# The third layer's attention: adding up the scan's states on POOL instead of DVE

## The chip, the cores and the metric

The kernel runs on one core of one Trainium2 chip. The metric is the device time of one execution in microseconds; three executions of the kernel before took 1468.19 us in the median (1460.56 to 1477.25). One more execution was recorded by the profiler; all rows in this document come from that one.

Engines are called as in the profile: PE (TensorE), PEld (its weight loads), DVE (VectorE), ACT (ScalarE), POOL (GpSimd), SP (SyncE, which issues DMAs here).

## What is computed

A stack of four layers on `x` of shape 4 x 256 x 256. Each layer adds a gated attention-like block and then a gated feed-forward block:

```python
x = x + jnp.tanh(g_xattn[1]) * _L1_xattn_ref(ctx_1024, _layernorm(x, axis=-1), ...)   # a state-space scan
x = x + jnp.tanh(g_ffn[1])   * _L1_ffn_ref(...)
x = x + jnp.tanh(g_xattn[2]) * _L2_xattn_ref(_layernorm(x, axis=-1), ctx_1024, ...)   # 16 heads of attention
x = x + jnp.tanh(g_ffn[2])   * _L2_ffn_ref(...)
x = x + jnp.tanh(g_xattn[3]) * _L3_xattn_ref(ctx_1024, _layernorm(x, axis=-1), ...)   # a second scan
x = x + jnp.tanh(g_ffn[3])   * _L3_ffn_ref(...)
```

The scan in layers 2 and 4 (`L1_`, `L3_`) depends on the context `ctx_1024` and its weights alone; only a gate at its end reads `x`:

```python
def step(state, inp):
    d, b, c, u = inp
    dA = jnp.exp(d[..., None] * A)
    state = state * dA + (d * u)[..., None] * b[:, None, :]
    y = jnp.einsum('bdn,bn->bd', state, c)      # 16 states n are summed for each channel d
    return (state, y)
y = y + D[None, :, None] * x
```

The attention of the third layer (`L2_xattn`) has 16 heads of width 128, 4 batches of 256 queries and 256 keys, with an RMS norm of queries and keys:

```python
q = rmsnorm(q, gq); k = rmsnorm(k, gk)
scores = jnp.einsum('bqhd,bkhd->bhqk', q, k) * scale
out = jnp.einsum('bhqk,bkhd->bqhd', jax.nn.softmax(scores, axis=-1), v)
return out.reshape(B, Sq, H * D) @ Wo
```

## The kernel before

There is no scheduler. Each engine has its own program, written out in order, and the engines meet at semaphores; a semaphore wait holds up all that stands behind it on its engine. What runs beside what is thus fixed by the order in which the lines stand and by the waits.

Since the last layer's scan needs nothing of `x`, it is laid into the third layer's attention (`m=1` in the `ssm_` functions). The scan has 32 groups (`GROUPS`): 4 batches x 4 blocks of 4 states x 2 halves of the 256 channels. Group `j` of a batch has block `j // 2` and half `c = j % 2`. A group is a tile of 128 partitions (channels) x 1024, four states (`NB`) by 256 positions (`S`). For each group:

- ACT makes the decays (L457), DVE the inputs by a product (L468), DVE runs the scan (L479, 1024 long);
- POOL multiplies the states by the rows of C (L499, in `ssm_hC`), into one of two buffers `ssm_hC_buf`;
- DVE adds up the four states (L520, a reduction of 1024 to 256 with strided input, into `ssm_part`) and adds the result to `ssm_y` (L524, 256 long). This is `ssm_reduce_dve`.

The attention goes through 64 steps, 16 heads times 4 batches, `step(i, k, b)` on PE, ACT and DVE alike; `h = 4*i + k` is the head. What this text calls **b0 to b3** are the four steps of a head. Each step, in order:

- PE: scores of this step (L1520); transposes of the weights of the step before (L1500); a piece of the next head's projections (keys and values L1442, queries L1451; in b3 the queries' sums of squares L1458 and the transposes of the keys L1466); values of the step before (L1508).
- DVE: row maxima (L1685), their scaled negatives (L1689), in b1 and b3 the scan's input product (L468), after ACT's exponentials (L1627) the reciprocal of the sums (L1695) and the normalization of the weights, two instructions of 128x256 (L1698), the copy of the step before's output (L1668), in b2 the keys' mean squares (L1659), in b3 the queries' (L1664). Then in b1 and b3 the scan; in b0 and b2 `ssm_reduce_dve` for the group whose scan ended the step before.
- POOL, once a head (`head` in `x_pool`): the product L499 of the even group; `rms`, the keys' inverse roots (L1753, 8 columns) and their application to the next head's keys (L1756, 1024 columns); `qrms`, the queries' inverse roots (L1762); the product L499 of the odd group.

The keys of the next head are transposed (L1466) only after L1756, and b0 of the next head can't take its maxima's scale before L1762. PE stands in order: the values of b2 (L1508) are behind that transpose.

Even heads from the third on (h = 2, 4, ..., 14) also carry the output projection of the pair of heads before them (PE L1490: 8 matmul records in b1, 16 in b2, 8 in b3; DVE adds them to `x`, L1674). They are called **projecting heads** below, the others **plain heads**.

The first batch of the scan runs beside heads 0 to 3, and so on. Heads 4 to 11 are a hardware loop on every engine.

Of the kernel before, what the change touches and what calls it, by code (L numbers as in the profile page):

```python
# [55 lines left out]
def flamingo_kernel(nc, A, out):  # L56
    with ExitStack() as ctx:
# [3 lines left out]
        def sem(name):  # L61
            return ctx.enter_context(nc.semaphore(name))
# [220 lines left out]
        s_ssm_y = sem("s_ssm_y")  # L283
        s_ssm_red = sem("s_ssm_red")
        s_ssm_red_y = sem("s_ssm_red_y")
        ssm_part = sb("ssm_part", [P, S])

        prep_groups += [
            ([win_rows[:, m, c, :] for m in range(2) for c in range(HC)], winT[:, :, :].rearrange("p a b -> p (a b)")),
# [220 lines left out]
                                        start=(g == 0 and n == 0), stop=(g == GB - 1 and n == NB - 1))  # L510
            last.then_inc(s_ssm_sum, 1)

        def ssm_reduce_dve(dve, m, b, j):

            c = j % HC
            q = b * GB * HC + j
            dve.wait_ge(s_ssm_hC, m * GROUPS + q + 1)
            if not (isinstance(b, int) and b == 0 and j == 0):
                dve.wait_ge(s_ssm_red_y, q)
            nc.vector.tensor_reduce(ssm_part[:, :], ssm_hC_buf[:, j % 2, :].rearrange("p (n l) -> p l n", n=NB),  # L520
                                    AX_X, ALU.add).then_inc(s_ssm_red, 1)
            dve.wait_ge(s_ssm_red, q + 1)
            row = ssm_y[:, m, ds(b, 1), c, :].rearrange("p a l -> p (a l)")
            nc.vector.tensor_tensor(row, row, ssm_part[:, :], ALU.add).then_inc(s_ssm_red_y, 1)  # L524

        def ssm_sum_dve(dve, m, b):
            dve.wait_ge(s_ssm_sum, m * GROUPS + (b + 1) * GB * HC)
# [17 lines left out]
        def gated_dve(dve, m, k):  # L545

            if m:
                norm_dve(dve, k)
                dve.wait_ge(s_ssm_red_y, GROUPS)
            else:  # L550
                norm_dve(dve, k)
                dve.wait_ge(s_ssm_y, B * HC)
            for b in range(B + 1):
                if b < B:
                    dve.wait_ge(s_z_silu, m * B + b + 1)
                    rows = z_gate[:, TPB * b:TPB * (b + 1), :]
                    nc.vector.tensor_tensor(rows, rows, ssm_y[:, m, b, :, :], ALU.mult).then_inc(s_z_prod, 1)
                if b:
                    dve.wait_ge(s_z_t, m * B + b)
                    rows = x[:, TPB * (b - 1):TPB * b, :].rearrange("p a n -> p (a n)")  # L560
                    nc.vector.scalar_tensor_tensor(out=rows, in0=bank[b % 2][:, :], scalar=tanh_g[:, 0, 2 * m + 1:2 * m + 2],
                                                   in1=rows, op0=ALU.mult, op1=ALU.add).then_inc(s_z_x, 1)
                    norm_stats(dve, range(TPB * (b - 1), TPB * b), s_z_x, m * B + b)
# [807 lines left out]
        x_nb = sb("x_nb", [P, 2, TPB])  # L1371
        x_sum = sb("x_sum", [P, 2, TPB])
        x_inv = sb("x_inv", [P, 2, TPB])
        s_x_g = sem("s_x_g")
        s_x_gqk = sem("s_x_gqk")
        s_x_w = [sem(f"s_x_w{r}") for r in range(2)]
# [6 lines left out]
        def after(eng, sem_, value):  # L1383

            if not (isinstance(value, int) and value <= 0):
                eng.wait_ge(sem_, value)

        def x_sp(sp):
            sp.dma_start(x_gqk[:, 0:1], A["L2_xattn_gq"].rearrange("(p a) -> p a", a=1)).then_inc(s_x_g, 16)
# [260 lines left out]
        def x_dve(dve):  # L1650
            V = nc.vector
            dve.wait_ge(s_x_g, 32)
            V.tensor_tensor(x_gqk[:, 0:1], x_gqk[:, 0:1], x_gqk[:, 1:2], ALU.mult).then_inc(s_x_gqk, 1)
            norm_dve(dve, 4)

            def krms(h):
                dve.wait_ge(s_x_ksq, 4 * h + 4)
                after(dve, s_x_rk, h)
                V.tensor_scalar(x_kve[:, :], x_kss[:, :], 1.0 / P, EPS, ALU.mult, ALU.add).then_inc(s_x_kve, 1)  # L1659

            def qrms(h):
                dve.wait_ge(s_x_ss, h + 1)
                after(dve, s_x_rq, h)
                V.tensor_scalar(x_qve[:, :], bank[2][:, 0:NT], L2_SCALE_EPS, None, ALU.add).then_inc(s_x_qve, 1)  # L1664

            def ocopy(s, r, b):
                dve.wait_ge(s_x_O, s + 1)
                V.tensor_copy(x_OT[:, r, b * S:(b + 1) * S], bank[7][:, 0:S]).then_inc(s_x_Oc, 1)  # L1668

            def add(n, p, at_bank):  # L1670
                dve.wait_ge(s_x_wo, n + 1)
                after(dve, s_x_add, n)
                rows = x[:, 2 * p:2 * p + 2, :].rearrange("p a n -> p (a n)")
                V.scalar_tensor_tensor(out=rows, in0=bank[at_bank][:, :], scalar=tanh_g[:, 0, 2:3], in1=rows,  # L1674
                                       op0=ALU.mult, op1=ALU.add).then_inc(s_x_add, 1)

            def step(i, k, b, first=False, final=False):
                h = i * HB + k
                s = i * (HB * B) + (k * B + b)
                par = b % 2  # L1680
                if b == 0:
                    dve.wait_ge(s_x_rq, h + 1)
                dve.wait_ge(s_x_S, s + 1)
                after(dve, s_x_exp, s - 1)
                V.tensor_reduce(x_top[:, par, :], bank[4 + par][:, :].rearrange("p (t n) -> p t n", t=TPB), AX_X, ALU.max,  # L1685
                                negate=True).then_inc(s_x_top, 1)
                dve.wait_ge(s_x_top, s + 1)
                for t in range(TPB):
                    last = V.tensor_scalar(x_nb[:, par, t:t + 1], x_top[:, par, t:t + 1],  # L1689
                                           x_rq[:, k % 2, TPB * b + t:TPB * b + t + 1], None, ALU.mult)  # L1690
                last.then_inc(s_x_max, 1)
                if par:
                    ssm_in_product(dve, 1, i, 2 * k + b // 2)
                dve.wait_ge(s_x_exp, s + 1)
                V.reciprocal(x_inv[:, par, :], x_sum[:, par, :]).then_inc(s_x_inv, 1)  # L1695
                dve.wait_ge(s_x_inv, s + 1)
                for t in range(TPB):
                    last = V.tensor_scalar(x_P[:, par, t * S:(t + 1) * S], x_P[:, par, t * S:(t + 1) * S],  # L1698
                                           x_inv[:, par, t:t + 1], None, ALU.mult)
                last.then_inc(s_x_P, 1)  # L1700
                if k % 2 == 0 and not (isinstance(h, int) and h < 2) and b == 1:
                    add(2 * h - 4, 0, 3)
                if not first:
                    r, pb = (k if b else k - 1) % 2, (b - 1) % B

                    u = i * (HB // 2) + (k if b else k - 1) // 2
                    after(dve, s_x_wo, 4 * u + (pb - 3))
                    ocopy(s - 1, r, pb)
                if not final:
                    n, r = h + 1, (k + 1) % 2  # L1710
                    if b == 2:
                        krms(n)
                    elif b == 3:
                        qrms(n)
                if k % 2 == 0 and not (isinstance(h, int) and h < 2):
                    u4 = 2 * h - 4
                    if b == 2:
                        add(u4 + 1, 1, 0)
                        add(u4 + 2, 2, 1)
                    elif b == 3:  # L1720
                        add(u4 + 3, 3, 3)
                j = 2 * k + b // 2
                if par:
                    ssm_scan(dve, 1, i, j)
                elif j:
                    ssm_reduce_dve(dve, 1, i, j - 1)
                elif not first:
                    ssm_reduce_dve(dve, 1, i - 1, GB * HC - 1)

            krms(0)  # L1730
            qrms(0)
            for k in range(HB):
                for b in range(B):
                    step(0, k, b, first=(k == 0 and b == 0))
            with dve.Fori(1, H // HB - 1) as i:
                for k in range(HB):
                    for b in range(B):
                        step(i, k, b)
            for k in range(HB):
                for b in range(B):  # L1740
                    step(H // HB - 1, k, b, final=(k == HB - 1))
            ssm_reduce_dve(dve, 1, B - 1, GB * HC - 1)
            after(dve, s_x_wo, 2 * H - 4)
            ocopy(H * B - 1, 1, B - 1)
            for p in range(4):
                add(2 * H - 4 + p, p, p)
                norm_stats(dve, (2 * p, 2 * p + 1), s_x_add, 2 * H - 3 + p)

        def x_pool(pool):
# [13 lines left out]

            def head(i, k, final=False):
                h = i * HB + k
                ssm_hC(pool, nc.gpsimd, 1, i, 2 * k)
                if not final:
                    rms(h + 1, (k + 1) % 2)
                    qrms(h + 1, (k + 1) % 2)
                ssm_hC(pool, nc.gpsimd, 1, i, 2 * k + 1)  # L1770

            rms(0, 0)
            qrms(0, 0)
# [84 lines left out]
                f = stop  # L1858

        def g_sp(sp):  # L1860
            sp.wait_ge(s_ssm_red_y, GROUPS)
            pad = FS2 // P * P
            sp.dma_start(g_wr[:, :], A["L2_ffn_Wr"]).then_inc(s_g_ld[0], 16)
            sp.dma_start(e_gw[:, :], A["L3_ffn_gate_w"]).then_inc(s_g_ld[0], 16)
# [644 lines left out]
```

## Time and profile before

| | |
|---|---|
| median of 3 executions | 1468.19 us (1460.56 to 1477.25) |
| the profiled execution | 1462.29 us, span of its trace 1460.6 us |
| busy over the span | PE 1153.7 us, DVE 905.0, ACT 627.8, POOL 577.9 |
| the attention with the scan in it | from about 540 to 992 us of the span |

The profile lists for each engine when each instruction started, how long it took and, in brackets, how long its engine had been idle before it and whose result ended that wait. The third layer's attention is nearly a third of the span. In it the work of one head comes back every 25 to 30 us, with the same instructions, so a few rows of one plain and one projecting head stand for all sixteen.

### The profile page before, as it was taken

Reading aid. Unit: us, or ns where it says so; the run is one execution under the profiler, and the core shown is the slowest. Engines: PE = TensorE matmul, PEld = TensorE weight load, DVE = VectorE, ACT = ScalarE, POOL = GpSimd, SP = SyncE. Lnnn points to the kernel's source line nnn. Section 1 sums busy time; section 2 is a strip of 40 time slices with the busy share of each in tenths; the row PEclk is TensorE's granted clock in tenths of the full one; section 3 lists DMA queues with packets and bytes.
Section 4 is the critical chain, followed back from the end, with each engine's and each line's share of the span. In section 5 each row is a group of like instructions: output and inputs, shape, how many; then the busy total and the mean of one; then the engine's idle time right before and its main releaser. Section 6 shows DMA issues by size and latency. Waiting matters only on the chain.

```text
span 1460.6 us, 18407 instructions
## 1 busy us (share of the span) xinstructions
PE 1153.7 (79%) x5364; PEld 875.7 (60%) x5365; DVE 905.0 (62%) x1598; ACT 627.8 (43%) x1682; POOL 577.9 (40%) x369
## 2 busy tenths in 40 slices
PE   6755687877448878889889889868999833999993
PEld 3545576665225556667677677646555532888782
DVE  4485998977698625887787888873222366232222
ACT  3382364543711136666666767635111014333331
POOL 1006888888001213343343443420000001788874
PEclk9687899988768987999899999979999956999997
DMA  5664799975300001022021022014600099455556
GB/s 164 158 134 113 206 314 270 267 180 95 115 1 1 29 14 37 30 80 71 11 80 68 12 79 72 2 42 145 159 0 1 10 272 216 86 83 82 82 81 125
DMA packets 130069, 145.61 MB, mean 100 GB/s; under 512 B 29510, under 2 KB 114239, under 8 KB 129991
## 3 DMA queue, kind: packets, MB, share of 16 engines
q1 hardware_dynamic: 104326, 110.05, 25.9%
q0 software_dynamic: 24576, 33.57, 13.7%
q10 hardware_dynamic: 1088, 1.05, 0.2%
q8 instruction: 36, 0.59, 0.2%
q14 instruction: 43, 0.34, 0.1%
HBM read 118.52 MB, written 26.12 MB: 99 GB/s over the span
## 4 chain that ended last, share of the span: by engine, by line
PE 40%; DVE 18%; issue 15%; POOL 9%; ACT 6%; DMA 5%; SPq 5%; DVEq 0%; ACTq 0%; POOLq 0%
PE bank L1904 6%; PE bank L2197 5%; DVE arena L479 4%; PE bank L1913 3%; PE bank L1490 3%; SPq L2083 2%; ACT arena L1627 2%; PE bank L1451 2%; DVE ssm_part L520 2%; POOL x_rq L1762 2%; PE bank L1442 2%; DVE x_top L1685 2%; DMA e_sums<-ctxT,put 2%; PE bank L1508 1%; PE bank L1264 1%
## 5 line engine op out<-in xcount | busy, mean ns | idle before, releaser
L479 DVE TENSOR_TENSOR_SCAN arena<-arena 128x1024 f32<-128x1024 f32 x64 | 146.5, 2289 | 12.4 <-issue 8.3
L499 POOL TENSOR_TENSOR arena<-arena 128x1024 f32<-128x1024 f32 x32 | 75.1, 2348 | 182.3 <-DVE arena L479 182.3
L913 POOL DMA_INDIRECT f_sums<-arena,put x64 | 123.3, 1927 | 24.0 <-issue 17.7
L200 POOL TENSOR_TENSOR rstd<-var_eps,minus_half 128x8 f32<-128x8 f32 x8 | 13.2, 1646 | 299.4 <-DVE var_eps L192 299.4
L1627 ACT ACTIVATE arena<-bank,x_nb,x_rq 128x256 f32<-128x256 f32 x128 | 71.1, 559 | 100.7 <-DVE x_nb L1689 100.7
L899 POOL DMA_INDIRECT arena<-y_rows,slots x64 | 83.2, 1300 | 77.8 <-DVEq L1108 57.6
L2197 PE MATMUL bank<-arena,ssm_y 128*128 x512 | 111.1, 360 | 2.6 <-issue 0.9
L2110 POOL DMA_INDIRECT e_sums<-ctxT,put x64 | 101.6, 1587 | 24.2 <-issue 16.7
L457 ACT ACTIVATE arena<-arena,ssm_A 128x255 f32<-128x255 f32 (+1 forms) x256 | 107.8, 499 | 1.8 <-DVE arena L429 1.8
L1904 PE MATMUL bank<-yT,arena 128*128 128x512 f32 (+1 forms) x224 | 102.4, 600 | 0.0
L509 PE MATMUL bank<-arena,ident 128*128 128x256 f32 x256 | 70.7, 424 | 38.4 <-DVE arena L499 34.0
L2197 PEld LDWEIGHTS bank<-arena,ssm_y 128*128 128x128 f32 x512 | 86.3, 192 | 10.9 <-issue 7.0
L2119 POOL DMA_INDIRECT y<-y_rows,slots x64 | 62.8, 982 | 73.7 <-DMA y_rows<-y 52.9
L2386 DVE TENSOR_SCALAR ctxT<-bank,slot_w 128x256 f32<-128x256 f32 x64 | 31.0, 484 | 94.5 <-DMA e_sums<-ctxT,put 80.2
L509 PEld LDWEIGHTS bank<-arena,ident 128*128 128x128 f32 x256 | 50.8, 207 | 56.1 <-DVE arena L499 36.3
L1508 PE MATMUL bank<-arena 128*128 128x256 f32 x256 | 77.0, 429 | 7.0 <-ACT arena L1617 7.0
L468 DVE TENSOR_TENSOR arena<-arena 128x1024 f32<-128x1024 f32 x64 | 77.9, 1218 | 0.0
L1520 PE MATMUL bank<-arena 128*128 128x256 f32 x256 | 74.6, 418 | 3.8 <-issue 1.6
L1508 PEld LDWEIGHTS bank<-arena 128*128 128x128 f32 x256 | 52.2, 214 | 31.1 <-ACT arena L1617 17.0
L1951 ACT ACTIVATE arena<-bank 128x512 f32<-128x512 f32 (+1 forms) x28 | 16.7, 597 | 122.6 <-PE bank L1904 122.6
L1904 PEld LDWEIGHTS bank<-yT,arena 128*128 128x128 f32 (+1 forms) x224 | 42.6, 191 | 42.9 <-issue 41.5
L1762 POOL TENSOR_TENSOR x_rq<-x_qve,minus_half 128x8 f32<-128x8 f32 x16 | 41.4, 2587 | 65.6 <-DVE x_qve L1664 65.6
(313 smaller groups left out, 2771.9 us busy)
## 6 DMA issues: line engine op xcount, KB each, us to landing
arena<-bc_rows SPq DMA_DIRECT2D x64, 512.0 KB
arena<-in_L_ffn_w_gate_dram SPq DMA_DIRECT2D x16, 256.0 KB
arena<-in_L_ffn_w_up_dram SPq DMA_DIRECT2D x16, 256.0 KB
arena<-in_L_ffn_w_down_dram SPq DMA_DIRECT2D x16, 256.0 KB
x<-in_L_ffn_w_gate_dram SPq DMA_DIRECT2D x16, 256.0 KB, 3.7
y<-in_L_ffn_w_up_dram SPq DMA_DIRECT2D x16, 256.0 KB, 4.0
yT<-in_L_ffn_w_down_dram SPq DMA_DIRECT2D x16, 256.0 KB, 4.6
arena<-in_L_ffn_Wd_dram SPq DMA_DIRECT2D x1, 3072.0 KB, 24.3
```

The lines of the kernel that those rows point to most:

```text
L457: last = nc.scalar.activation(ssm_decay[:, j % 2, n * S + 1:(n + 1) * S], ssm_delta[:, c, ds(b * S + 1, S - 1)], ACT.Exp, scale=ssm_A[:, m ...
L468: nc.vector.tensor_tensor(ssm_in.rearrange("p (n l) -> p n l", n=NB), ssm_B[:, g % 2, :].rearrange("p (n l) -> p n l", n=NB), ssm_du[:, c, ...
L479: nc.vector.tensor_tensor_scan(ssm_h[:, j % 2, :], ssm_decay[:, j % 2, :], ssm_in, 0.0, ALU.mult, ALU.add).then_inc(s_ssm_h, 1)
L499: ops.tensor_tensor(ssm_hC_buf[:, j % 2, :], ssm_h[:, j % 2, :], ssm_C[:, g % 2, :], ALU.mult).then_inc(s_ssm_hC, 1)
L509: last = nc.tensor.matmul(bank[6 + c][:, 0:S], ident[:, :], ssm_hC_buf[:, j % 2, n * S:(n + 1) * S], start=(g == 0 and n == 0), stop=(g == ...
L899: nc.gpsimd.indirect_dma_start(out=f0_xg[:, n % RING, e, :], out_offset=None, in_=y_rows, in_offset=bass.IndirectOffsetOnAxis(ap=slots[:, ...
L913: nc.gpsimd.indirect_dma_start(out=f0_sums[m % SUMS], out_offset=bass.IndirectOffsetOnAxis(ap=put[:, m:m + 1], axis=0), in_=f0_ye[:, n % R ...
L1508: last = nc.tensor.matmul(bank[7][:, 0:S], x_kv[:, NT * r + TPB * b + j, P:2 * P], x_PT[:, b % 2, j * S:(j + 1) * S], start=(j == 0), stop ...
L1627: last = nc.scalar.activation(x_P[:, b % 2, t * S:(t + 1) * S], bank[4 + b % 2][:, t * S:(t + 1) * S], ACT.Exp, bias=x_nb[:, b % 2, t:t + ...
L1904: last = nc.tensor.matmul(bank[2 * (t % 2) + w][0:rows, :], wt[:, c * D + h * rows:c * D + (h + 1) * rows], yT[:, h, n * HALF:(n + 1) * HA ...
L2110: nc.gpsimd.indirect_dma_start(out=e_sums[t % 2], out_offset=bass.IndirectOffsetOnAxis(ap=put[:, t:t + 1], axis=0), in_=e_ye[:, t % 4, :], ...
L2197: last = nc.tensor.matmul(dst, e_xgT[:, r, h * P:(h + 1) * P], src[:, ds(which, 1), h, :].rearrange("p a (w n) -> p (a w) n", w=2), start= ...
```

## The change

The sum over four states goes from DVE to POOL, and is gathered per batch and half in an accumulator `ssm_acc` of 256 columns. Behind each product L499 POOL now adds the upper 512 columns of the buffer to the lower 512, then the two quarters that are left to the accumulator: one addition of 256 for the first block of a batch (`j < 2`), two for the others. DVE adds the accumulators to `ssm_y` once for each batch and half: at the end of b1 of heads 4, 8 and 12, and at the end of the stage. `ssm_part` is gone; `ssm_acc` lies in a part of the arena that the attention doesn't use otherwise. Three waits count 8 additions to `ssm_y` in place of 32.

```diff
+        def ssm_out_pool(pool, m, b, j):
             c = j % HC
             q = b * GB * HC + j
+            ssm_hC(pool, nc.gpsimd, m, b, j)
+            pool.wait_ge(s_ssm_hC, m * GROUPS + q + 1)
+            add = nc.gpsimd.tensor_tensor
+            both = ssm_hC_buf[:, j % 2, 0:2 * S]
+            add(both, both, ssm_hC_buf[:, j % 2, 2 * S:4 * S], ALU.add).then_inc(s_ssm_half[0], 1)
+            after(pool, s_ssm_half, q + 1)
+            parts = ssm_hC_buf[:, j % 2, 0:S], ssm_hC_buf[:, j % 2, S:2 * S]
+            acc = ssm_acc[:, c, :]
+            if j < HC:
+                after(pool, s_ssm_red_y, b * HC)
+                add(acc, parts[0], parts[1], ALU.add).then_inc(s_ssm_red, 1)
+            else:
+                pool.wait_ge(s_ssm_red, q - 1)
+                add(acc, acc, parts[0], ALU.add).then_inc(s_ssm_some[0], 1)
+                after(pool, s_ssm_some, b * (GB - 1) * HC + (j - HC + 1))
+                add(acc, acc, parts[1], ALU.add).then_inc(s_ssm_red, 1)
+
+        def ssm_out_dve(dve, m, b):
+
+            for c in range(HC):
+                dve.wait_ge(s_ssm_red, b * GB * HC + (GB - 1) * HC + c + 1)
+                row = ssm_y[:, m, ds(b, 1), c, :].rearrange("p a l -> p (a l)")
+                nc.vector.tensor_tensor(row, row, ssm_acc[:, c, :], ALU.add).then_inc(s_ssm_red_y, 1)
...
                 if par:
                     ssm_scan(dve, 1, i, j)
-                elif j:
-                    ssm_reduce_dve(dve, 1, i, j - 1)
-                elif not first:
-                    ssm_reduce_dve(dve, 1, i - 1, GB * HC - 1)
+                if b == 1 and k == 0 and not (isinstance(i, int) and i == 0):
+                    ssm_out_dve(dve, 1, i - 1)
...
-            ssm_reduce_dve(dve, 1, B - 1, GB * HC - 1)
+            ssm_out_dve(dve, 1, B - 1)
...
-                ssm_hC(pool, nc.gpsimd, 1, i, 2 * k)
+                ssm_out_pool(pool, 1, i, 2 * k)
                 if not final:
                     rms(h + 1, (k + 1) % 2)
                     qrms(h + 1, (k + 1) % 2)
-                ssm_hC(pool, nc.gpsimd, 1, i, 2 * k + 1)
+                ssm_out_pool(pool, 1, i, 2 * k + 1)
```

On POOL, from the product of an even group to that of the next even group, before (L1753 and L1756 are `rms`, L1762 `qrms`):

```order
L499 TENSOR_TENSOR arena<-arena 128x1024 [waits s_ssm_red,s_ssm_C1,s_ssm_h]
L1753 TENSOR_TENSOR x_rk<-x_kve,minus_half 128x8 [waits s_x_khat,s_x_kve]
L1756 TENSOR_TENSOR arena<-arena,x_rk 128x8x128 [waits s_x_rk]
L1762 TENSOR_TENSOR x_rq<-x_qve,minus_half 128x8 [waits s_x_exp,s_x_qve]
L499 TENSOR_TENSOR arena<-arena 128x1024 [waits s_ssm_red,s_ssm_C1,s_ssm_h]
```

and the same stretch now (the product is at L498, the new additions at L520, L529 and L531, the norms at L1771, L1774 and L1780):

```order
L498 TENSOR_TENSOR arena<-arena 128x1024 [waits s_ssm_red,s_ssm_C1,s_ssm_h]
L520 TENSOR_TENSOR arena<-arena 128x512 [waits s_ssm_hC]
L529 TENSOR_TENSOR arena<-arena 128x256 [waits s_ssm_red,s_l0_out]
L531 TENSOR_TENSOR arena<-arena 128x256 [waits s_l0_att]
L1771 TENSOR_TENSOR x_rk<-x_kve,minus_half 128x8 [waits s_x_khat,s_x_kve]
L1774 TENSOR_TENSOR arena<-arena,x_rk 128x8x128 [waits s_x_rk]
L1780 TENSOR_TENSOR x_rq<-x_qve,minus_half 128x8 [waits s_x_exp,s_x_qve]
L498 TENSOR_TENSOR arena<-arena 128x1024 [waits s_ssm_red,s_ssm_C1,s_ssm_h]
L520 TENSOR_TENSOR arena<-arena 128x512 [waits s_ssm_hC]
L529 TENSOR_TENSOR arena<-arena 128x256 [waits s_ssm_red,s_l0_out]
L531 TENSOR_TENSOR arena<-arena 128x256 [waits s_l0_att]
```

The three additions of the even group now stand between its product and the keys' norm; those of the odd group stand behind its product, at the end of the head.

On DVE, from b2's normalization to b3's maxima, before:

```order
L1698 TENSOR_SCALAR arena<-arena,x_inv 128x256 [waits s_x_inv]
L1698 TENSOR_SCALAR arena<-arena,x_inv 128x256
L1668 COPY arena<-bank 128x256 [waits s_x_O]
L1659 TENSOR_SCALAR x_kve<-x_kss 128x8 [waits s_x_rk,s_x_ksq]
L520 TENSOR_REDUCE ssm_part<-arena 128x256 [waits s_ssm_red_y,s_ssm_hC]
L524 TENSOR_TENSOR ssm_y<-ssm_y,ssm_part 128x256 [waits s_ssm_red]
L1685 TENSOR_REDUCE x_top<-bank 128x2 [waits s_x_exp,s_x_S]
```

and now:

```order
L1718 TENSOR_SCALAR arena<-arena,x_inv 128x256 [waits s_x_inv]
L1718 TENSOR_SCALAR arena<-arena,x_inv 128x256
L1688 COPY arena<-bank 128x256 [waits s_x_O]
L1679 TENSOR_SCALAR x_kve<-x_kss 128x8 [waits s_x_rk,s_x_ksq]
L1705 TENSOR_REDUCE x_top<-bank 128x2 [waits s_x_exp,s_x_S]
```

The reduction and the addition to `ssm_y` are gone from b2, and likewise from b0. Both stood behind the instruction that releases POOL's keys' norm (L1659), not ahead of it.

## Rows read from the trace of the kernel before

**Rows 1.** Busy time by engine in the attention (--windows; busy us, instructions, mean granted clock, DMA)

```profile
565.00:985.00 420.00, 362.98 (x1670) 280.92 (x1669) 340.99 (x620) 266.30 (x803) 167.61 (x77) 0.91 0.15 48
```

**Rows 2.** Groups by line and shape, 565 to 985 us: busy us, mean ns | idle before, releasers

```profile
L499 POOL TENSOR_TENSOR arena<-arena 128x1024 f32<-128x1024 f32 x32 | 75.1, 2348 | 182.3 <-DVE arena L479 182.3
...
L520 DVE TENSOR_REDUCE ssm_part<-arena 128x256 f32<-128x1024 f32 x32 | 62.0, 1939 | 2.5 <-POOL arena L499 2.5
...
L468 DVE TENSOR_TENSOR arena<-arena 128x1024 f32<-128x1024 f32 x31 | 37.7, 1216 | 0.0
```

**Rows 3.** Timeline of POOL in a plain head: start us, us, instruction [idle before]

```profile
697.85 2.35 POOL L499 TENSOR_TENSOR arena<-arena 128x1024 f32<-128x1024 f32 x1 [9.12 <-DVE arena L479]
701.22 1.64 POOL L1753 TENSOR_TENSOR x_rk<-x_kve,minus_half 128x8 f32<-128x8 f32 x1 [1.01 <-DVE x_kve L1659]
702.93 1.90 POOL L1756 TENSOR_TENSOR arena<-arena,x_rk 128x1024 f32<-128x1024 f32 x1
709.53 3.59 POOL L1762 TENSOR_TENSOR x_rq<-x_qve,minus_half 128x8 f32<-128x8 f32 x1 [4.70 <-DVE x_qve L1664]
```

**Rows 4.** Timeline of DVE in the same head, b2, b3 and the next b0

```profile
700.11 0.61 DVE L1698 TENSOR_SCALAR arena<-arena,x_inv 128x256 f32<-128x256 f32 x2
...
700.98 0.16 DVE L1659 TENSOR_SCALAR x_kve<-x_kss 128x8 f32<-128x8 f32 x1
...
703.03 2.08 DVE L524 TENSOR_TENSOR ssm_y<-ssm_y,ssm_part 128x256 f32 x1
705.03 0.68 DVE L1685 TENSOR_REDUCE x_top<-bank 128x2 f32<-128x512 f32 x1
...
705.99 1.22 DVE L468 TENSOR_TENSOR arena<-arena 128x1024 f32<-128x1024 f32 x1
...
708.66 0.42 DVE L1668 COPY arena<-bank 128x256 f32<-128x256 f32 x1 [0.49 <-PE bank L1508]
...
713.31 0.69 DVE L1685 TENSOR_REDUCE x_top<-bank 128x2 f32<-128x512 f32 x1 [1.62 <-POOL x_rq L1762]
```

**Rows 5.** Timeline of PE: the keys' transposes and the projections, in three heads

```profile
717.01 3.37 PE L1490 MATMUL bank<-arena 128*128 128x256 f32 x8
...
760.20 1.97 PE L1466 MATMUL bank<-ident,arena 128*128 128x128 f32 x8 [1.69 <-POOL arena L1756]
...
772.30 3.37 PE L1490 MATMUL bank<-arena 128*128 128x256 f32 x8
...
790.16 1.07 PE L1466 MATMUL bank<-ident,arena 128*128 128x128 f32 x8
...
791.93 1.89 PE L1490 MATMUL bank<-arena 128*128 128x256 f32 x8
```

**Rows 6.** Timelines of POOL, DVE and PE: a projecting head, then the plain head's b0, b1

```profile
786.32 1.64 POOL L1753 TENSOR_TENSOR x_rk<-x_kve,minus_half 128x8 f32<-128x8 f32 x1 [0.99 <-DVE x_kve L1659]
788.04 1.90 POOL L1756 TENSOR_TENSOR arena<-arena,x_rk 128x1024 f32<-128x1024 f32 x1
...
793.52 0.42 DVE L1668 COPY arena<-bank 128x256 f32<-128x256 f32 x1
...
799.29 0.62 DVE L1698 TENSOR_SCALAR arena<-arena,x_inv 128x256 f32<-128x256 f32 x2
...
803.90 1.03 PE L1508 MATMUL bank<-arena 128*128 128x256 f32 x4
...
805.98 2.28 DVE L479 TENSOR_TENSOR_SCAN arena<-arena 128x1024 f32<-128x1024 f32 x1
```

**Rows 7.** Timelines of POOL and DVE beside each other, second layer's feed-forward

```profile
459.18 2.84 POOL L1340 TENSOR_TENSOR arena<-l_mask,l_v 128x1024 f32<-128x1024 f32 x1 [14.00 <-DVE l_v L1313]
...
459.02 1.21 DVE L416 TENSOR_TENSOR arena<-arena 128x1024 f32<-128x1024 f32 x1
460.26 2.83 DVE L417 TENSOR_TENSOR arena<-arena 128x1024 f32<-128x1024 f32 x1
463.13 0.69 DVE L419 TENSOR_SCALAR arena<-arena 128x1024 f32<-128x1024 f32 x1
```

More of the change, by code:

```diff
@@ L285, in flamingo_kernel @@
         s_ssm_red_y = sem("s_ssm_red_y")
-        ssm_part = sb("ssm_part", [P, S])
         prep_groups += [
@@ L511, in ssm_pe @@
             last.then_inc(s_ssm_sum, 1)
-        def ssm_reduce_dve(dve, m, b, j):
+        def ssm_out_pool(pool, m, b, j):
             c = j % HC
             q = b * GB * HC + j
[L517 to L524, printed above, removed]
+            ssm_hC(pool, nc.gpsimd, m, b, j)
[19 more added lines that the diff above has]
+                nc.vector.tensor_tensor(row, row, ssm_acc[:, c, :], ALU.add).then_inc(s_ssm_red_y, 1)
         def ssm_sum_dve(dve, m, b):
@@ L548, in gated_dve @@
                 norm_dve(dve, k)
-                dve.wait_ge(s_ssm_red_y, GROUPS)
+                dve.wait_ge(s_ssm_red_y, B * HC)
             else:
@@ L1373, in flamingo_kernel @@
         x_inv = sb("x_inv", [P, 2, TPB])
+        ssm_acc = area(2 * NT * 2 * P + NT * P, HC, S)
+        assert 2 * NT * 2 * P + NT * P + HC * S <= l1_free + 2 * AR + K1 * A1
+        s_ssm_half, s_ssm_some = (s_l0_out, B), (s_l0_att, B)
         s_x_g = sem("s_x_g")
@@ L1385, in after @@
             if not (isinstance(value, int) and value <= 0):
-                eng.wait_ge(sem_, value)
+                if isinstance(sem_, tuple):
+                    eng.wait_ge(sem_[0], sem_[1] + value)
+                else:
+                    eng.wait_ge(sem_, value)
         def x_sp(sp):
@@ L1860, in g_sp @@
         def g_sp(sp):
-            sp.wait_ge(s_ssm_red_y, GROUPS)
+            sp.wait_ge(s_ssm_red_y, B * HC)
             pad = FS2 // P * P
```

## The prediction

> **What bounds the kernel now.** I first read the busy times of the attention stage [rows 1]. Of 420 us PE is busy for 363, DVE for 341, ACT for 266, POOL for 168. PE and DVE look full, POOL has room, and the change takes load from DVE (32 reductions of 1.94 us, [rows 2]) to POOL. Shares do not say what ends last, so next came the timelines of one plain head, engine by engine.
>
> They show a ring that passes through POOL. In b2 DVE makes the keys' mean squares at 700.98 [rows 4]. POOL, idle for 1.01 us until then, starts L1753 at 701.22 and L1756 at 702.93 [rows 3]. PE waits for L1756 (in the head shown for PE for 1.69 us, [rows 5]), transposes the keys, and only then computes the values of b2, which stand behind. DVE's copy of these values waits 0.49 us for PE and starts at 708.66; the queries' mean squares, the scan, POOL's L1762 (709.53) and the next head's maxima (713.31, after 1.62 us idle) follow [rows 3, 4]. So in a plain head every microsecond that L1756 comes later goes on the path. The reduction stands behind the instruction that releases POOL, so it is not ahead of L1756. It delays only b3's maxima, and b3 then waits for PE anyway.
>
> A projecting head is tighter packed. L1756 ends at 789.94 [rows 6] and PE, full of projections, reaches the transposes at 790.16 without a wait [rows 5]. The copy at 793.52 starts without a wait too [rows 6]: there DVE is last, by 1.4 us over PE, whose values are done when L1490 starts, at 791.93, or just after [rows 5].
>
> **Second reading: who blocks whom.** Two operations with both inputs in SBUF do not run at once on DVE and POOL. DVE's L416 began at 459.02; POOL's L1340, begun at 459.18, took 2.84 us in place of 1.9, and DVE's next, L417, ready at 460.26, took 2.83 in place of 1.22 [rows 7, 2]. POOL's turn lay between them: whoever waits gets the next turn, and the other waits the whole of it. The same is seen in L524, which took 2.08 us for 256 columns because L1756 had begun 0.10 us before [rows 3, 4], and in L1762, 3.59 us behind a scan.
>
> **The change, part by part** (over the profiled execution, 1462.3 us):
>
> *Length of the additions.* Together they have 512 + 256 + 256 = 1024 columns, as L499, 2.35 us [rows 2]. Each waits for the one before; that gap is 702.93 - 701.22 - 1.64 = 0.07 us [rows 3], three times: 2.56 us. Bounds: 2.1 us at L1756's rate (1.90 for 1024, plus the gaps), 3.0 if each had a fixed part of 0.15 on top. I take 2.6, since L499 has the same two full inputs.
>
> *A. Plain heads, even group, 8 heads.* L499 ends at 700.20; L1753 would start at 702.8 instead of 701.22: +1.6. DVE adds to that. Without the reduction b3's maxima start about when the reduction did, at 701.05, and the product L468 0.96 us later [rows 4], at 702.0, when POOL is in its second addition (701.5 to 702.1). The product takes the next turn, 1.2 us, and the third addition follows: L1753 at 704.0, +2.8. If DVE is held up before that (C), the product comes behind the third addition and short waits remain, about +1.9. Taken: 8 x 1.9 = +15.2 with C, 22.4 without.
>
> *B. Projecting heads, even group, 7.* POOL's idle time before L1753 is 0.99 [rows 6], so L1756 ends 1.6 to 2.9 us later, at 791.5 to 792.8; transposes and values take 1.8 more: 793.3 to 794.7, against the copy's 793.52. DVE itself, without reduction, would be ready by 791.2. So 0 to +1.2; 0.4 for four of them, +1.6. In the other three (heads 4, 8, 12) DVE's new rows come right behind the scan of b1 and meet L499: the second of them waits as L524 did, but for 2.35 us, and the keys' mean squares behind it too. The copy's slack eats about half: 3 x 1.2 = +3.6 (bounds 0 and 8).
>
> *C. Normalization of b0.* In b2 L1698 starts at 700.11 and L499 ends at 700.20 [rows 3, 4]; after the odd group's scan the distance in b0 is the same. Before, POOL was idle from there on; now its 512-column addition starts within 0.1 us of L1698. L1698 has one tensor input, which rows 7 do not price. But L419, also with one input, takes 0.69 us for 1024 columns where two inputs take 1.22 [rows 7, 2], thus reads two columns at a time, and I take it that it needs what a second input needs. Then L1698 waits for 1.2 us (one addition) to 1.8 (its second instruction waits for the next addition as well); 0 if the two don't meet. Taken: 1.5, in 15 b0 = +22.5. PE's transposes wait for exactly this. In b2 the same wait is covered by A, since POOL's norm is late anyway.
>
> The Trainium skill has this as a rule ("SBUF — State Buffer", section "SBUF: two separate sides"): a VectorE instruction in a two-port mode, or with two SBUF inputs, and a GpSimd instruction that reads SBUF hold the shared port pair exclusively and in full. Rows 7 agree for two inputs; for the one-input form no row here shows it, and by the page C is due, without it C is 0.
>
> *D. What is saved.* In b0 reduction and row addition are on DVE's path in a plain head: normalization at 799.29, scan of b1 at 805.98 [rows 6]. PE comes right behind: its values end at 803.90 + 1.03 = 804.93, the copy takes 0.42, so the scan can start at 805.35. Saved: 0.6 of 2.3 us, 8 times, -4.8. In a projecting head b1's eight projection records stand ahead of those values and PE is last: 0. In b2 the saving is covered by L1756 (A, B).
>
> *E. The end of the stage.* There 2.6 us of POOL take the place of a reduction of 1.94 on the way to the next stage's loads: +0.6.
>
> *F. The clock.* The same eight records L1490 took 3.37 us in two projecting heads and 1.89 in the third shown [rows 5]; L1466 took 1.97 behind a wait and 1.07 without. That is a factor of 1.8, near the two levels 1.2 and 2.4 GHz; the stage's mean grant is 0.91 [rows 1]. Both waits of PE grow, so I count five more slow projecting heads at 1.8 us (1.5 in L1490 and a little around it): +9.
>
> Sum: 15.2 + 1.6 + 3.6 + 22.5 - 4.8 + 0.6 + 9 = +47.7, **1510** for a profiled execution. The median of the runs before lies 5.9 us above the profiled one (1468.2 against 1462.3), so **1516** for the median.
>
> **The rivals.** A measurement of this kernel can tell about 1% (15 us) from no change.
>
> 1. *One-input operations don't wait for POOL.* C is 0, A becomes 22.4, B 4.8 + 3.6, F some 4: 22.4 + 8.4 - 4.8 + 0.6 + 4 = +30.6, **1499**. For it: L1698 never ran beside POOL. Against: its rate.
> 2. *The clock falls at every wait.* Then the 8 plain b0 and the 7 projecting transposes also pay 1.8 us: +27 on top, **1543**. For it: two heads of seven fell at waits not longer than these will be. Against: PE's work per head is unchanged, and in plain heads L1466 runs slow already without harm downstream.
> 3. *The additions nearly fit.* They take 2.1 us, the product misses their gaps, one-input operations don't wait: A 8 x 1.1 = 8.8, B 3.6, D -4.8, E 0.6: +8.2, **1476**, within 1%.
> 4. *DVE is what bounds, and its relief wins.* If each head were set by DVE's sum, the 2.3 us of b0 would come back 15 times: -34, **1434**. It decides if POOL's additions end within its 1.0 us of idle time before L1753, and if PE has the room that rows 6 deny it (0.6 us). For it: DVE busy 341 of 420. Against: three additions of 2.1 us at least.
> 5. That the change doesn't do what it says is excluded by the order of instructions: the reductions are gone, the additions are there.
>
> **Numbers.** Chances: forecast 0.45, rival 1 0.25, rival 2 0.16, rival 3 0.10, rival 4 0.04. Likeliest 1516. The forecast's own range, with C at 1.2 to 1.8, A at 1.6 to 2.8 and F at 0 to 20, is 1500 to 1535. With rivals 1 and 2 and their bounds the range is 1484 to 1550; left out are rivals 3 and 4 and the far end of 2. Faster by over 1%: 0.04 (rival 4). Within 1%: 0.10 (rival 3). Slower by over 1%: 0.86.
>
> **What would show it.** A: L1753 no longer waits for DVE but follows an addition directly, 1.6 to 3 us later against its product; PE's wait before L1466 grows from 1.7 to over 3 us, and appears in projecting heads. A product L468 of 2 us or more, or a third addition of some 1.8 us, is their meeting. C: L1698 with a longest time of 1.2 to 1.8 us in place of 0.35; if it stays at 0.35 beside running additions, rival 1 holds. D: in plain heads DVE waits for PE before b1's copy. F: more heads with L1490 near 3.4 us for eight records, mean clock under 0.91. Wrong altogether I would be if L1753 still waited for DVE, which needs additions of 1.0 us in all.

## The result and the profile after

The changed kernel took 1539.47 us in the median of four executions (1534.82 to 1542.62), the kernel before 1469.52 us, also of four (1460.56 to 1477.25). The ratio is 1.0476, 95% interval 1.0409 to 1.0542: 70 us slower. The forecast was 1516, the range 1484 to 1550.

The profiled execution has a span of 1538.5 us. To see where the difference lies, take the stretch from the first keys' norm L1756 of the attention (L1774 now) to the last one, fifteen heads later, and read the busy times in it. Columns: stretch, its length, busy us of PE, PEld, DVE, ACT, POOL (instructions), mean granted clock, DMA. Before:

```profile
544.76:946.84 402.08, 357.32 (x1640) 277.82 (x1641) 317.86 (x583) 265.92 (x807) 160.58 (x75) 0.92 0.16 50
```

and after:

```profile
542.05:1012.94 470.89, 382.72 (x1652) 305.42 (x1653) 301.87 (x537) 270.80 (x808) 238.75 (x153) 0.86 0.13 43
```

The stretch is 68.8 us longer, nearly the whole loss. DVE gave up what lies in it of the reductions and of the additions behind them (28 of each, 79.5 us together) and is busy for only 16 us less; POOL got 78 us more; PE is busy for 25 us more although its work is nearly the same (12 more records fall into the stretch), and the mean clock went from 0.92 to 0.86.

PE's idle time in it went from 45 to 88 us. Two lines of PE hold most of that, the transposes of the weights and those of the keys (last column: idle before them, and what ended it). Before:

```profile
L1500 PE MATMUL bank<-ident,arena 128*128 128x128 f32 x232 | 38.0, 288 | 22.5 <-DVE arena L1698 22.5
...
L1466 PE MATMUL bank<-ident,arena 128*128 128x128 f32 x120 | 22.4, 347 | 14.0 <-POOL arena L1756 14.0
```

and after:

```profile
L1520 PE MATMUL bank<-ident,arena 128*128 128x128 f32 x236 | 39.0, 291 | 61.2 <-DVE arena L1718 61.2
...
L1486 PE MATMUL bank<-ident,arena 128*128 128x128 f32 x120 | 28.4, 415 | 20.1 <-POOL arena L1774 20.1
```

So by far the most of the new waiting ends with DVE's normalization, not with the keys' norm.

Some groups of the stage by line and shape, 565 to 1065 us (busy us, mean ns | idle before), to be laid beside [rows 2]:

```profile
L1718 DVE TENSOR_SCALAR arena<-arena,x_inv 128x256 f32<-128x256 f32 x124 | 89.0, 759 | 2.2
...
L520 POOL TENSOR_TENSOR arena<-arena 128x512 f32<-128x512 f32 x32 | 42.5, 1329 | 2.5
...
L467 DVE TENSOR_TENSOR arena<-arena 128x1024 f32<-128x1024 f32 x31 | 41.9, 1353 | 0.1
```

L1718, DVE's normalization, has a mean of 759 ns; in the kernel before it was 350. That is 51 us of waiting counted as busy, and it eats more than half of what the removed reductions and additions freed.

POOL in a plain head, to be laid beside [rows 3]:

```profile
782.32 2.35 POOL L498 TENSOR_TENSOR arena<-arena 128x1024 f32<-128x1024 f32 x1 [6.36 <-DVE arena L478]
784.75 1.39 POOL L520 TENSOR_TENSOR arena<-arena 128x512 f32<-128x512 f32 x1
786.22 0.73 POOL L529 TENSOR_TENSOR arena<-arena 128x256 f32<-128x256 f32 x1
787.03 0.73 POOL L531 TENSOR_TENSOR arena<-arena 128x256 f32<-128x256 f32 x1
787.71 1.65 POOL L1771 TENSOR_TENSOR x_rk<-x_kve,minus_half 128x8 f32<-128x8 f32 x1
789.44 1.90 POOL L1774 TENSOR_TENSOR arena<-arena,x_rk 128x1024 f32<-128x1024 f32 x1
795.85 3.46 POOL L1780 TENSOR_TENSOR x_rq<-x_qve,minus_half 128x8 f32<-128x8 f32 x1 [4.51 <-DVE x_qve L1684]
```

L1771 has no bracket: it follows the third addition instead of waiting 1.01 us for DVE. It starts 3.04 us after the product's end; before it was 1.02. DVE in the same head (b2, b3, next b0), beside [rows 4]:

```profile
784.67 1.63 DVE L1718 TENSOR_SCALAR arena<-arena,x_inv 128x256 f32<-128x256 f32 x2
...
786.55 0.43 DVE L1679 TENSOR_SCALAR x_kve<-x_kss 128x8 f32<-128x8 f32 x1
...
789.41 2.33 DVE L1718 TENSOR_SCALAR arena<-arena,x_inv 128x256 f32<-128x256 f32 x2
795.18 0.42 DVE L1688 COPY arena<-bank 128x256 f32<-128x256 f32 x1 [3.43 <-PE bank L1528]
...
802.12 1.78 DVE L1718 TENSOR_SCALAR arena<-arena,x_inv 128x256 f32<-128x256 f32 x2
```

The pair L1718 took 0.61 before (700.11, [rows 4]). In b2 (784.67) it meets L520, in b0 (802.12) L520 and the addition behind it, and in b3 (789.41) the keys' norm L1774 itself. Even the norm of 8 columns, L1679, takes 0.43 in place of 0.16. PE in the same stretch, beside [rows 5]:

```profile
791.39 1.97 PE L1486 MATMUL bank<-ident,arena 128*128 128x128 f32 x8 [2.70 <-POOL arena L1774]
...
803.96 1.12 PE L1520 MATMUL bank<-ident,arena 128*128 128x128 f32 x4 [3.38 <-DVE arena L1718]
804.87 2.81 PE L1510 MATMUL bank<-arena 128*128 128x256 f32 x8
```

PE waits 2.70 us for the keys here, and 3.38 for b0's weights, after which the projections L1510 take 2.81 where 1.89 is full speed. The wait for the keys is no good measure of the loss: over the eight plain heads of the stretch it comes to 14.0 us before and 13.7 now (2.70 is the longest, 0.73 the shortest). What grew there is the wait just ahead of it, for b2's weights, from 0.7 to between 1.8 and 2.1 us in every plain head. The keys' norm is late by about as much, so the two waits together grew by 1.3 us a head. The wait for b0's weights, in b1, went from 1.0 to 2.3 us in plain heads (head 1 apart) and from 0.3 to 2.1 us before to 3.3 to 4.1 us in projecting ones, 27.5 us more in all.

In a projecting head the keys' norm is late as well, and in four of the seven DVE's product gets ahead of it. First POOL, then DVE, then PE:

```profile
885.48 2.90 POOL L1774 TENSOR_TENSOR arena<-arena,x_rk 128x1024 f32<-128x1024 f32 x1
```

```profile
885.41 1.22 DVE L467 TENSOR_TENSOR arena<-arena 128x1024 f32<-128x1024 f32 x1
```

```profile
888.43 1.82 PE L1486 MATMUL bank<-ident,arena 128*128 128x128 f32 x8 [1.84 <-POOL arena L1774]
```

In the other three (heads 4, 8 and 12) POOL has only two additions to do, since the group is the first block of its batch. There the product waits for L1774 (2.47 us at 822.34), and PE waits only 0.25 us for the keys. In all seven PE also waits 0.4 to 1.3 us ahead of the queries' sums of squares (L1478) for DVE's addition to `x` (L1694), 5.0 us in all; before, it didn't.

### The profile page after: what moved, and what is told of

Read it like the earlier page. It is cut to its first block, busy times and chain, and to the rows that moved or that the text cites. A ratio compares the mean times of both kernels' runs of the same rounds, so it can differ in the third digit from the quotient of the medians.

```text
span 1538.5 us, 18446 instructions
## 1 busy us (share of the span) xinstructions
PE 1185.4 (77%) x5364; PEld 908.9 (59%) x5365; DVE 883.5 (57%) x1542; ACT 632.4 (41%) x1682; POOL 670.9 (44%) x457
## 4 chain that ended last, share of the span: by engine, by line
PE 34%; POOL 21%; issue 17%; DVE 10%; DMA 7%; SPq 5%; ACT 4%; another core or an unknown queue 1%; DVEq 0%; POOLq 0%; ACTq 0%
PE bank L1922 5%; POOL f_sums L927 5%; POOL arena L913 4%; DVE arena L478 3%; PE bank L2215 3%; PE bank L1931 3%; PE bank L1462 3%; PE bank L1510 3%; SPq L2101 2%; PE bank L1528 2%; POOL arena L1774 2%; POOL x_rq L1780 2%; PE bank L1471 2%; DMA f_sums<-arena,put 2%; POOL arena L498 2%
## 5 line engine op out<-in xcount | busy, mean ns | idle before, releaser
L498 POOL TENSOR_TENSOR arena<-arena 128x1024 f32<-128x1024 f32 x32 | 75.7, 2367 | 173.0 <-DVE arena L478 173.0
L1520 PE MATMUL bank<-ident,arena 128*128 128x128 f32 x256 | 43.4, 296 | 66.7 <-DVE arena L1718 66.7
L1718 DVE TENSOR_SCALAR arena<-arena,x_inv 128x256 f32<-128x256 f32 x128 | 90.2, 746 | 2.2
L467 DVE TENSOR_TENSOR arena<-arena 128x1024 f32<-128x1024 f32 x64 | 82.2, 1284 | 0.2 <-issue 0.2
L1520 PEld LDWEIGHTS bank<-ident,arena 128*128 128x128 f32 x256 | 32.6, 151 | 82.0 <-DVE arena L1718 77.5
L1688 DVE COPY arena<-bank 128x256 f32<-128x256 f32 x64 | 26.7, 418 | 84.9 <-PE bank L1528 84.9
L1510 PE MATMUL bank<-arena 128*128 128x256 f32 x256 | 70.4, 432 | 5.0 <-DVE arena L1688 5.0
```

Source lines behind the costliest of these rows:

```text
L498: ops.tensor_tensor(ssm_hC_buf[:, j % 2, :], ssm_h[:, j % 2, :], ssm_C[:, g % 2, :], ALU.mult).then_inc(s_ssm_hC, 1)
L1510: last = nc.tensor.matmul(bank[to][:, t * D:(t + 1) * D], x_OT[:, e, (2 * p + t) * P:(2 * p + t + 1) * P], x_wo[:, e, :], start=(e == 0), ...
```

## The experiments

All but experiment 9 start from the changed kernel and take away, move or add one or two things. Times were measured on three chips, on which the kernel before had medians of 1467.82, 1465.63 and 1460.81 us, so ratios are what to compare; 0.0068 is 10 us.

**1. No additions at all.** Their place is taken by increments of the semaphores, and the accumulators are zeroed once.

```diff
-            add = nc.gpsimd.tensor_tensor
-            both = ssm_hC_buf[:, j % 2, 0:2 * S]
...
-                add(acc, acc, parts[1], ALU.add).then_inc(s_ssm_red, 1)
+            pool.sem_inc(s_ssm_half[0], 1)
+            if j >= HC:
+                pool.sem_inc(s_ssm_some[0], 1)
+            pool.sem_inc(s_ssm_red, 1)
```

> Neither engine adds up the four states: all 32 groups of additions on POOL are left out (the accumulators are set to zero once), DVE stays relieved. What is left is the relief alone. Theory (POOL's ring and PE bound the stage, DVE's reduction was mostly covered): 1465 us, between 1458 and 1475, against 1469.5 before. Rival (the relief is worth its 2.3 us in each b0, and the additions cost that much more): 1436 us.

Measured: 1473.69 us, ratio 1.0047 (1.0023 to 1.0071). The relief of DVE by itself gains nothing; it costs some 7 us. DVE is busy for 270 us of 425 in the stage and often waits for PE. Measured from keys' norm to keys' norm, five of the eight plain heads are 0.4 to 0.7 us shorter than before, but the seven projecting heads are 12.8 us longer together. PE before a plain head's b1 and before a projecting head's b1:

```profile
743.85 0.66 PE L1510 MATMUL bank<-ident,arena 128*128 128x128 f32 x4 [1.33 <-DVE arena L1708]
...
769.57 0.68 PE L1510 MATMUL bank<-ident,arena 128*128 128x128 f32 x4 [2.22 <-DVE arena L1708]
770.07 3.58 PE L1500 MATMUL bank<-arena 128*128 128x256 f32 x8
```

In all seven projecting heads these eight records take 3.0 to 3.6 us, behind waits of 2.2 to 2.5 us; before, two of seven were that slow [rows 5].

**2. The same time on POOL, hardly any SBUF.**

```diff
-            add = nc.gpsimd.tensor_tensor
...
+            for n in range(2):
+                nc.gpsimd.tensor_tensor(ssm_fill[:, n, 0:7], ssm_fill[:, 2, 0:7], minus_half[:, 0:7], ALU.pow)
```

> In place of the additions POOL does two powers on 7 columns per group, about 3.0 us together, as long as the three additions, but hardly touching SBUF; the sum is left out. It has the delay of the keys' norm (A), not the meeting with DVE's normalization (C). Theory: A without C, 1495 us (1485 to 1510). Rival 'time on POOL is all that counts': 1539, as the change. Rival 'only the meeting on SBUF counts': 1466, as with no additions.

Measured: 1498.94 us, ratio 1.0214 (1.0174 to 1.0254): 1498 on the scale of a kernel before of 1467. Of the 63 us between no additions and the change, time alone makes 24 (0.0167), the rest, 38 us (0.0262), comes with the operands in SBUF. The 24 us are the later keys' norm: against experiment 1 the stretch of fifteen heads is 25.1 us longer, PE's wait for the keys grew from 14.6 to 39.0 us, its wait for the weights (32.9 and 32.1) did not grow, and it is busy for 1 us more. POOL's rows and DVE's beside them:

```profile
759.77 2.98 POOL L520 TENSOR_TENSOR ssm_fill<-ssm_fill,minus_half 128x7 f32<-128x7 f32 x2
```

```profile
759.60 0.62 DVE L1711 TENSOR_SCALAR arena<-arena,x_inv 128x256 f32<-128x256 f32 x2
...
761.44 1.21 DVE L468 TENSOR_TENSOR arena<-arena 128x1024 f32<-128x1024 f32 x1
```

DVE's normalization and its product run at their usual 0.62 and 1.21 while POOL computes powers. What stops them in the change is not that POOL is busy but what the additions do in SBUF. (Reading and writing are not told apart by this run.)

**3 and 4. Half of the additions.** Only those of the even groups (`if j % 2 == 1` the increments of experiment 1 and `return`), then only those of the odd ones; the others' sums are left out.

> Only the even groups are added up (the additions ahead of the keys' norm); those of the odd groups are left out. Theory: step A and the meetings of b2 and b3, 1500 us (1490 to 1515). If A is nothing and all comes from b0: 1466.

Measured: 1504.90 us, ratio 1.0250 (1.0198 to 1.0301).

> Only the odd groups are added up (beside b0, after the product at the head's end); those of the even groups are left out. The keys' norm isn't delayed. Theory: step C in b0, 1.5 to 2 us in 15 heads less 5 us, with the clock: 1500 us (1488 to 1512). Rival 'only A counts': 1466.

Measured: 1505.39 us, ratio 1.0236 (1.0202 to 1.0270). Over the kernel without additions the even groups cost 0.0203 (30 us), the odd ones 0.0189 (28 us); together 58 us of the 63. So the two places cost about the same, and add up within the intervals. In the profiled stretch of the first, against experiment 1, PE idles 18 us longer and is busy for 8 more; of the second, 18 and 9, the idle time all before the transposes of the weights (32.9 to 52.1 us). With odd groups only, b0 looks like this on DVE and then on PE:

```profile
850.23 1.88 DVE L1724 TENSOR_SCALAR arena<-arena,x_inv 128x256 f32<-128x256 f32 x2
```

```profile
852.16 1.12 PE L1526 MATMUL bank<-ident,arena 128*128 128x128 f32 x4 [3.91 <-DVE arena L1724]
853.07 3.62 PE L1516 MATMUL bank<-arena 128*128 128x256 f32 x8
```

The direct delay is 1.88 - 0.62 = 1.3 us. PE's wait is 3.91 us (2.2 to 2.5 in experiment 1), and the projections behind it run at the lower clock throughout: 3.62 in place of 1.89.

**5. Even group's additions behind the keys' norm.**

```diff
-                ssm_out_pool(pool, 1, i, 2 * k)
+                ssm_hC(pool, nc.gpsimd, 1, i, 2 * k)
                 if not final:
                     rms(h + 1, (k + 1) % 2)
+                ssm_out_pool(pool, 1, i, 2 * k)      # the additions alone
+                if not final:
                     qrms(h + 1, (k + 1) % 2)
```

(Here and in experiments 6 and 7 the product `ssm_hC` is taken out of `ssm_out_pool` and stands ahead of it, the odd group's too.)

> All additions are kept, but those of the even group stand behind the keys' norm (L1771, L1774), where POOL is idle for over 4 us before it needs the queries' squares; those of the odd group stay. Theory: step A and the meeting of b2 are gone, the meeting in b0 stays as in the kernel with odd groups alone (1505): 1508 us (1498 to 1522). Rival 'POOL's time in the ring counts wherever it stands': 1539.

Measured: 1506.19 us, ratio 1.0276 (1.0235 to 1.0318).

**6. Odd group's additions behind b0's normalization.**

```diff
-                ssm_out_pool(pool, 1, i, 2 * k + 1)
+                ssm_hC(pool, nc.gpsimd, 1, i, 2 * k + 1)
+                if not final:
+                    pool.wait_ge(s_x_P, 4 * h + 5)
+                ssm_out_pool(pool, 1, i, 2 * k + 1)      # the additions alone
```

> All additions are kept where the change has them, but those of the odd group wait until DVE has normalized b0's weights, so they no longer meet it. Theory: step C in b0 is gone, A stays as with even groups alone (1505): 1506 us (1496 to 1520). If the meeting with L1718 is not what the odd groups cost: 1539.

Measured: 1508.45 us, ratio 1.0297 (1.0280 to 1.0314). Each move alone takes back 0.018 to 0.020 of 0.0476, with all additions done and no instruction less.

**7. Both moves.**

> Both: the even group's additions behind the keys' norm, the odd group's behind the normalization of b0. All the work of the change is done. Theory: nearly all of the loss comes back, 1480 us (1470 to 1495); not below the 1474 with no additions at all, so no faster than before.

Measured: 1482.64 us, ratio 1.0132 (1.0105 to 1.0160). 50 of the 70 us are back. POOL in the middle of a plain head and at the next b0:

```profile
766.43 1.32 POOL L519 TENSOR_TENSOR arena<-arena 128x512 f32<-128x512 f32 x1
...
777.21 1.27 POOL L519 TENSOR_TENSOR arena<-arena 128x512 f32<-128x512 f32 x1 [1.21 <-DVE arena L1717]
```

The first stands behind the keys' norm, the second waits for b0's normalization, which is back at 0.61 us. The additions still meet DVE in two places: the product L467 in b1, beside which POOL's 256-column addition L528 takes 1.6 to 1.7 us instead of 0.73, and b3's normalization, whose pair takes 2.0 us. PE's waits do not show them: for the weights 32.2 us in the stretch of fifteen heads, for the keys 15.6, as in experiment 1 (32.9 and 14.6).

**8. Needless products of PE ahead of its waits, in the changed kernel.** Five products of 256 columns each, into banks that are free there.

```diff
+            def keep_warm(at, n):
+                for _ in range(n):
+                    nc.tensor.matmul(bank[at][:, 0:S], ident[:, :], ctxT[:, 0:S], start=True, stop=True)
...
+                pe.wait_ge(s_x_kvc, 4 * h + 4)
+                keep_warm(0, 5)
                 pe.wait_ge(s_x_khat, h + 1)
...
-                pe.wait_ge(s_x_P, s + 1)
                 after(pe, s_x_PTc, s)
+                keep_warm(6, warm)                   # 5 in b1, where b0's weights are awaited, else 0
+                pe.wait_ge(s_x_P, s + 1)
```

> The change with five needless products of 256 columns put ahead of each wait of PE for the keys' norm and of each wait for b0's normalization (some 2.2 us of PE each at full clock), so that PE does not stand idle there. The results aren't used. Theory (F): the clock falls less often after these waits; 1520 us (1508 to 1535) against 1539. If the clock costs nothing: 1539 to 1545, the needless products being covered by the waits; if they aren't covered, more.

Measured: 1526.25 us, ratio 1.0421 (1.0401 to 1.0441). That is 8 us less than the change, with more work on PE, but the two intervals overlap. The mean clock in the stretch of fifteen heads went from 0.86 to 0.94, and L1516 shows the full speed behind the wait:

```profile
801.45 0.66 PE L1526 MATMUL bank<-ident,arena 128*128 128x128 f32 x4 [1.48 <-DVE arena L1724]
801.94 1.89 PE L1516 MATMUL bank<-arena 128*128 128x256 f32 x8
```

The 8 us are not what the clock cost. PE is busy for 420.6 us of this stretch, 90.8 of them with needless products, so its own work takes about 330 us in place of 383. But the needless products took 90.8 us while PE's idle time fell only from 88 to 39 us: most of what the clock gave back went into products that ran past the waits.

**9 to 11. The same with fewer needless products** (three ahead of the keys' norm in plain heads, four in b1 of projecting heads), in the kernel before, in the one without additions, and in the one with both moves.

> The kernel before with needless products of 256 columns ahead of two waits of PE: three ahead of the keys' norm in plain heads, four ahead of b0's normalization in projecting heads. Theory: in the kernel before the clock fell hard in two projecting heads (about 2.3 us each) and behind the keys' norm in plain heads, where the slack of b3 covers it: 1463 us (1455 to 1469) against 1468, perhaps too little to tell. If needless products only delay: 1470 or more.

Measured: 1456.66 us against 1460.81, ratio 0.9983 (0.9955 to 1.0010): no difference that can be told.

> No additions on either engine (their sum is left out), with the same needless products. With no additions DVE's relief gained 0.7 us in plain heads and lost 2 in projecting ones, where the records L1500 (the projections) ran at half speed behind a longer wait. If the clock is what ate the relief: 1458 us (1450 to 1466), under the 1474 without these products by over 10. If not: 1472.

Measured: 1450.16 us, ratio 0.9938 (0.9914 to 0.9962), 0.0109 (16 us) below the same kernel without the products. PE in a projecting head's b1, to be laid beside the rows of experiment 1:

```profile
753.46 1.89 PE L1467 MATMUL bank<-ctxT,ident 128*128 128x256 f32 x8
756.10 0.66 PE L1517 MATMUL bank<-ident,arena 128*128 128x128 f32 x4 [0.75 <-DVE arena L1715]
756.60 1.89 PE L1507 MATMUL bank<-arena 128*128 128x256 f32 x8
```

The needless records L1467 fill the wait; the projections behind it run at 1.89 us instead of 3.58. So with these products the relief of DVE no longer costs: the kernel is 9 us below the kernel before, and about 7 below experiment 9, which has the same products (those two intervals just overlap).

> All additions at the two late places, with the same needless products: the one version with the change's work that might equal or beat the kernel before. Theory: 1468 us (1460 to 1478), against 1483 without the products; not faster than before by 1%.

Measured: 1462.11 us, ratio 0.9998 (0.9973 to 1.0023), the kernel before to within the interval. This is the best version with the change's work found here; none beat the kernel before.

The length of the stretch of fifteen heads and its mean clock, from the busy times of each profiled execution:

| kernel | stretch, us | clock | ratio of the times |
|---|---|---|---|
| before | 402.1 | 0.92 | 1 |
| the change | 470.9 | 0.86 | 1.0476 |
| 1 no additions | 414.1 | 0.90 | 1.0047 |
| 2 powers in their place | 439.3 | 0.89 | 1.0214 |
| 3 even groups only | 440.0 | 0.89 | 1.0250 |
| 4 odd groups only | 440.7 | 0.86 | 1.0236 |
| 5 even moved | 440.1 | 0.87 | 1.0276 |
| 6 odd late | 440.0 | 0.89 | 1.0297 |
| 7 both | 413.7 | 0.90 | 1.0132 |
| 8 change, PE kept busy | 460.0 | 0.94 | 1.0421 |
| 9 before, PE kept busy | 397.7 | 0.97 | 0.9983 |
| 10 no additions, PE kept busy | 396.3 | 0.96 | 0.9938 |
| 11 both, PE kept busy | 404.1 | 0.95 | 0.9998 |

## Why the prediction was right, and where its sizes were off

The direction and both places of loss held, and experiments 2 to 7 show the causes. The size did not hold so well: the sum was +47.7, measured were +70. The time lies above the forecast's own range (1500 to 1535), and inside 1484 to 1550 because that range took in rival 2, whose 1543 is the nearest value. What follows lays the terms beside the stretch of fifteen heads, where PE idles 43.4 us longer and is busy for 25.4 more.

- *Length of the additions.* Taken 2.6 us with their gaps. The rows of POOL give 1.39 + 0.73 + 0.73 and gaps of about 0.08, 3.0 us, the upper bound. Each addition has a fixed part of some 0.2 us (an estimate from 1.26 for 512 columns and 0.73 for 256), which L499 alone could not show. The prediction also took three additions for every group; the 8 groups of a first block have two.
- *A, plain heads.* Taken +1.9 a head, 15.2 in all; the keys' norm starts 2.0 us later against the product's end, as forecast. The product of b3 (787.86) came behind the third addition, as forecast for the case that DVE is held up. PE's two waits of b3 (b2's weights, keys) grew by 10.4 us over the eight heads. The sign that was named, over 3 us before L1466, did not come, since most of the delay shows in the wait ahead of it.
- *B, projecting heads.* Undersized. The keys' norm is up to 1.9 us later here too, and in four heads the product, taken as harmless, starts 0.07 us ahead of L1774, which then lasts 2.90. Heads 4, 8 and 12, on which most of the term was laid, wait least for the keys. PE's waits in b3, those for L1694 among them, grew by 11.8 us in the stretch, against 5.2 taken.
- *C, normalization of b0.* The step stood on an analogy: one-input operations of 0.69 us for 1024 columns need what a second input needs. They do. The pair takes 1.6 us in b0 of plain heads (2.04 in head 1) and 1.75 to 2.04 in that of projecting ones, against 0.62: a direct wait of 1.2 us in the mean, the lower end of 1.2 to 1.8. PE's wait for b0's weights is 18 us longer than in experiment 1; C was put at 22.5. With what PE is busy longer behind these waits, the odd groups cost 28 us. Experiment 6 took back 26 us by moving just the odd group's additions. The rule cited from the Trainium skill ("SBUF — State Buffer", "SBUF: two separate sides") agrees with the trace in this form too: 1.53 to 2.34 us for the pair L1718 and 0.43 for L1679 beside POOL's additions, 0.62 and 0.16 without. In experiment 2 the trace does not agree that the ports are held in full for a whole instruction of POOL: DVE ran at its usual pace inside POOL's powers on 7 columns, and there the measurement decides.
- *A meeting that was missed.* In b3 the normalization meets L1774 (2.33 us for the pair), since b3 now runs early. DVE's copy still waits 3.43 us for PE behind it, so it costs nothing.
- *D, the relief.* Put at -4.8 for the plain heads and 0 for the projecting ones. By experiment 1 it is right for most plain heads (0.4 to 0.7 us each) and wrong for the projecting ones, which became 12.8 us longer: PE waits longer for b0's weights there and runs the projections behind at 3.0 to 3.6 us. Experiment 10 shows that this goes with the clock: with PE kept busy the seven take 191.4 us together, against 210.4 in experiment 1 and 197.6 before.
- *F, the clock.* The term most undersized. Taken +9, five more slow projecting heads. These came (seven now show L1510 at some 3 us), but the keys' transposes L1486 in projecting heads (1.57 to 1.97 us, 1.07 before) and PE's other lines pay too: PE is busy for 25.4 us more in the stretch.
- *Rivals.* The one-input rival is out: L1718 did not stay at 0.35. "DVE is what bounds" is out by experiment 1. "The additions nearly fit" is out: they take 3.0 us, and L1771 waits for DVE in only three of the fifteen heads, each with two additions. Rival 2, the clock at every wait (1543), is nearest in time and in part right: it laid 36 us on the clock, the forecast 9, and the stretch shows 25. Experiment 8 can't decide between them, as its products cost more than the waits they filled.

What stays open: how the 30 us of the even groups divide. By experiment 2 the later keys' norm alone makes about 24 us, with hardly any loss of clock (its powers take 3 us in the first blocks too, so this is rather high). With real additions the waits stand elsewhere and PE is busy for 8 us more; how much of that is the meetings with DVE, and how much the clock behind each wait, no run separates.

## What to carry to other kernels

Moving work from DVE to POOL gains only where DVE was what the others waited for, and here it cost wherever POOL's additions stood beside DVE's products or its normalization. Look at where on POOL's queue the work goes: the same additions cost 70 us where they were put and 19 us a few instructions later. And look at what waits behind: here a PE that was handed its operands a microsecond or two later came out of some waits at half its clock, and its busy time grew by 25 us beside 43 us of waiting.

## What the runs showed of the hardware

- POOL's powers on 7 columns and its additions on 512 last about alike (1.5 and 1.3 us), but only the additions hold up DVE: busy time on POOL does not tell how it holds up DVE.
- Where they meet, DVE and POOL take turns, instruction by instruction. In b0 the two L1718 and POOL's additions interleave: L1718 waits for L520, then its second for L529 (802.12 to 803.90).
- Taking work off DVE made PE slower: with the relief alone the mean clock in the stretch fell from 0.92 to 0.90, and the stretch grew by 12 us (the whole execution by some 7 in the median). Needless products in PE's waits raised it to 0.96 and the stretch fell to 396 us.
- An added product on PE can be free: in the kernel before, seven products of 256 columns in each pair of heads changed the time by a ratio of 0.9983, and 1 lies inside the interval (0.9955 to 1.0010).
